# The gate's eight columns carried through the wide products of a graph, scan and expert kernel, and new banks and a new place for the heads' exponents

## What is computed

```python
x1 = x  + softmax(mask(leaky(s1 + s2.T), adj)) @ wh      # wh = LN(x) @ W, s = wh @ a
x2 = x1 + mamba2(LN(x1)) @ W_lin + b_lin                 # 8 heads, decay matrices exp(cs_i - cs_j)
x3 = x2 + sum_r (adj == r) @ LN(x2) @ weight[r] + bias   # 4 relations
logits = LN(x3) @ gate_w + gate_b                        # 8 experts
out = x3 + prob * expert(LN(x3))                         # top 1 with a capacity, 256 -> 1024 -> 256
```

## Time and profile before

| | |
|---|---|
| median of 3 runs | 3670.32 us (3669.29 to 3671.39) |
| profiled execution | 3668.25 us |
| its span, first to last instruction | 3666.5 us |
| mean granted TensorE clock | 0.99 of full speed |
| busy: PE / weight loads / DVE / ACT / POOL | 95% / 77% / 70% / 48% / 49% of the span |
| first phase, 64 graphs | 0 to about 2620 us, a pair of rounds in 79.8 us |
| second phase, 71 tiles | 2637 us to the end |

### The profile page before, as it was taken

How to read it: one execution, slowest core, us unless ns; L and a number is a source line. 1 busy time by engine, 2 the same in 40 slices (tenths; PEclk the granted TensorE clock), 3 DMA queues, 4 the chain that set the end, 5 groups by cost and what they waited for, 6 DMA issues and landing times.

```text
span 3666.5 us, 64685 instructions
## 1 busy us (share of the span) xinstructions
PE 3470.5 (95%) x20028; PEld 2838.1 (77%) x20028; DVE 2562.8 (70%) x7429; ACT 1776.8 (48%) x3627; POOL 1808.5 (49%) x2010
## 2 busy tenths in 40 slices
PE   7999999999999999999999999999699999999998
PEld 5777777777777777777777777777488888888887
DVE  5878888887888888788888878888444444444444
ACT  4556655655655555565565556555232323323232
POOL 3545554454554545545454554545354555545453
PEclk8999999999999999999999999999799999999999
DMA  3121111111111111111111111111155555556563
GB/s 104 39 46 36 35 40 43 37 42 41 37 38 40 40 37 46 37 37 40 37 42 35 46 37 37 40 38 33 58 199 194 196 190 193 193 192 197 194 196 128
DMA packets 166001, 301.92 MB, mean 82 GB/s; under 512 B 37376, under 2 KB 138240, under 8 KB 147776
## 3 DMA queue, kind: packets, MB, share of 16 engines
q0 software_dynamic: 38272, 196.40, 15.7%
q1 hardware_dynamic: 91536, 70.58, 6.3%
q10 hardware_dynamic: 36144, 34.35, 6.0%
HBM read 248.61 MB, written 52.65 MB: 82 GB/s over the span
## 4 chain that ended last, share of the span: by engine, by line
PE 51%; DVE 26%; POOL 12%; issue 8%; ACT 1%; DVEq 0%; DMA 0%; ACTq 0%; POOLq 0%; SPq 0%
PE bank L1337 13%; PE bank L1351 13%; PE bank L1083 7%; POOL masks L466 7%; DVE conv L798 6%; PE bank L1101 5%; PE bank L1189 4%; DVE y L966 3%; PE bank L1289 3%; DVE y L971 2%; POOL row L452 2%; POOL rstd L452 2%; DVE stats L779 2%; DVE xn L789 1%; PE bank L1220 1%
## 5 line engine op out<-in xcount | busy, mean ns | idle before, releaser
L732 ACT ACTIVATE decay<-bank,w_up 128x256 f32<-128x256 f32 x568 | 269.4, 474 | 700.3 <-PE bank L1337 694.5
L1083 PE MATMUL bank<-xn1T,w_in 128*128 128x256 f32 x2304 | 523.4, 381 | 15.3 <-issue 14.3
L1337 PE MATMUL bank<-zs,w_up 128*128 128x256 f32 x2272 | 504.6, 380 | 0.6 <-ACT zs L590 0.6
L1351 PE MATMUL bank<-w_dn,decay 128*128 128x256 f32 x2272 | 502.1, 379 | 0.0
L1101 PE MATMUL bank<-w_rel,hT 128*128 128x256 f32 x2048 | 492.7, 384 | 0.0
L1083 PEld LDWEIGHTS bank<-xn1T,w_in 128*128 128x128 f32 x2304 | 434.1, 190 | 72.3 <-issue 14.0
L798 DVE SCALAR_TENSOR_TENSOR conv<-bank,conv_w,conv 128x255 f32<-128x255 f32 (+2 forms) x960 | 461.3, 481 | 34.8
L1337 PEld LDWEIGHTS bank<-zs,w_up 128*128 128x128 f32 x2272 | 433.4, 191 | 60.3 <-issue 0.9
L1351 PEld LDWEIGHTS bank<-w_dn,decay 128*128 128x128 f32 x2272 | 426.2, 190 | 55.1
L1044 DVE TENSOR_TENSOR hT<-bank,w_dn 128x256 f32<-128x256 f32 x142 | 60.3, 424 | 537.1 <-PE bank L1351 537.1
L1101 PEld LDWEIGHTS bank<-w_rel,hT 128*128 128x128 f32 x2048 | 368.9, 190 | 62.8 <-ACT hT L590 13.0
(11 more groups left out here) (219 smaller groups left out, 6341.4 us busy)
## 6 DMA issues: line engine op xcount, KB each, us to landing
token_rows<-row SPq DMA_DIRECT2D x64, 258.0 KB, 2.7
xT_sb<-in_xT ACTq DMA_DIRECT2D x64, 256.0 KB
x_sb<-in_x ACTq DMA_DIRECT2D x64, 256.0 KB, 2.7
adj_sb<-in_adj SPq DMA_DIRECT2D x64, 256.0 KB, 3.0
adjt_sb<-in_adjT SPq DMA_DIRECT2D x64, 256.0 KB, 3.0
out<-row SPq DMA_DIRECT2D x64, 256.0 KB, 2.2
w_in<-token_rows,idc POOLq DMA_INDIRECT x142
out<-hT,ids POOLq DMA_INDIRECT x142
```

Source lines behind the costliest of these rows:

```text
L732: nc.scalar.activation(hid(f), bank[f % 4][:, 0:GROUP], ACT.Relu, bias=b1[q % 2][:, f:f + 1]).then_inc(hid_ready, 1)
L1083: ins = mm(dst, w_in[:, k, first:first + P], xn1T[:, k, :], start=k == 0, stop=k == DK - 1)
L1337: ins = mm(bank[f % 4][:, 0:GROUP], w1[i][:, k, f * P:(f + 1) * P], xgT[:, k, :], start=k == 0, stop=k == DK - 1)
L1351: ins = mm(bank[4 + j][:, 0:D], hid(f)[:, j * P:(j + 1) * P], w2[i][:, f, :], start=f == 0, stop=f == FB - 1)
```

## The change

Three things are done.

1. **The gate rides along.** A tile that held D = 256 columns now holds GX = 264 (x, x1, x1b, x2, x2b, wh, w_gat, w_lin, w_proj, w_rel, b_lin, b_rel, row). The eight further columns of each weight are that weight times the centred gate matrix, made once at the start with transposed copies of the weights. So x3's columns 256 to 263 are x3 @ gwc, and the logits come from two small DVE operations. xn3, its turns, xn3T and the gate product are gone. The DRAM row grows from 260 to 268 floats.
2. **Banks.** Each head has its own entry in EXPO; relate(1) goes to bank 7, the attention product to banks 0 and 1, the projection's second half to bank 2.
3. **Order.** `expo(range(0, 4))` stands in front of the turns of prob on the PE, and probT between decays 1 and 2 on ACT.

The core of the diff (loads, semaphores and slices `[..., 0:D]` left out):

```diff
-    EXPO = (2, 5, 3, 4)
+    EXPO = (2, 5, 1, 3, 4, 2, 5, 3)
...
-        WS = D + 2
+        WS = GX + 2 + E
...
         gat_loads = [
-            (w_gat, by_tile(io["L0_gnn_W"])),
+            (gate_w, by_tile(io["L1_ffn_gate_w"])),
+            (w_gat[:, :, 0:D], by_tile(io["L0_gnn_W"])),
+            (w_gatT, by_tile(io["gnn_WT"])),
             (a_bc, io["L0_gnn_a"].rearrange("(a d) o -> (a o) d", a=2).partition_broadcast(P)),
...
         # scalar engine
                     need(act, hp_made, b1_)
+                    need(act, x1_ready, b1_)
                     for t in range(T):
-                        ins = nc.scalar.activation(wh[:, t, :], bank[t][:, 0:D], ACT.Copy, scale=rstd[0][:, t:t + 1])
+                        copy(x[:, t, D:GX], bank[t][:, GX + 2:WS])
+                        ins = nc.scalar.activation(wh[:, t, :], bank[t][:, 0:GX], ACT.Copy, scale=rstd[0][:, t:t + 1])
...
-                    act.wait_ge(prob_turned, b1_ + 1)
-                    need(act, hp_made, b1_)
-                    copy(probT[:], bank[0][:, :]).then_inc(probT_ready, 1)
-                if b2_ is not None:
-                    for h in range(H):
+                for h in range(H):
+                    if h == 2 and b1_ is not None:
+                        act.wait_ge(prob_turned, b1_ + 1)
+                        need(act, hp_made, b1_)
+                        copy(probT[:], bank[0][:, :]).then_inc(probT_ready, 1)
+                    if b2_ is not None:
                         act.wait_ge(expo_made, 8 * b2_ + h + 1)
...
-                if b3_ is not None:
-                    act.wait_ge(xn3_turned, b3_ + 1)
-                    copy(xn3T[:], bank[7][:, :]).then_inc(xn3T_ready, 1)
...
         # vector engine
+                if is_first(b2_):
+                    dve.wait_ge(more_made, 1)
+                    v.tensor_copy(w_rel[:, :, :, D:GX], bank[6][:, REL:REL + R * DK * E].rearrange(
+                        "p (r k e) -> p r k e", r=R, k=DK))
+                    v.tensor_copy(w_proj[:, :, D:GX], ...).then_inc(more_ready, 1)
...
                 if b3_ is not None:
-                    need(dve, xn3_turned, b3_)
-                    normalise(3, xn3, row[:, :, 0:D], xn3_ready, b3_)
+                    dve.wait_ge(rstd_ready[3], b3_ + 1)
+                    for t in range(T):
+                        ins = v.scalar_tensor_tensor(lg[:, T * turn_[1] + t, :], row[:, t, D:GX], row[:, t, GX + 1:GX + 2],
+                                                     gate_b[:, t, :], ALU.mult, ALU.add)
+                    ins.then_inc(lg_in, 1)
...
-                    dve.wait_ge(gate_made, b3_ + 1)
                     g_, i, n = turn_
-                    ins = v.tensor_tensor(lg[:, T * i:T * (i + 1), :], bank[6]..., gate_b[:], ALU.add)
...
         # tensor engine, once, before the first product
+            for k in range(DK):
+                ins = mm(bank[6][:, 0:E], ones_row[:, 0:P], gate_w[:, k, :], start=k == 0, stop=k == DK - 1)
+            ins.then_inc(gate_sum_made, 1)
...
+            pe.wait_ge(gwc_ready, 1)
+            for i in range(DK):
+                for k in range(DK):
+                    ins = mm(bank[6][:, (1 + i) * E:(2 + i) * E], w_gatT[:, k, i * P:(i + 1) * P], gwc[:, k, :], ...)
+            ins.then_inc(gat_more_made, 1)
+            pe.wait_ge(gat_more_ready, 1)
+            for k in range(DK):
+                ins = mm(bank[4][:, D:GX], ones_row[:, 0:P], w_gat[:, k, D:GX], ...)
+            ins.then_inc(more_sum_made, 1)
...
                 if t == 0:
                     pe.wait_ge(xt_in, 16 * (b + 1))
-                    need(pe, probT_ready, b)
-                else:
                     need(pe, x1_ready, b)
...
-                    elif h in (2, 3):
-                        pe.wait_ge(xdt_ready, 2 * b + h - 1)
+                    elif h == 2:
+                        if b1_ is not None:
+                            pe.wait_ge(wh_ready, b1_ + 1)
+                    elif h in (3, 4):
+                        pe.wait_ge(xdt_ready, 2 * b + h - 2)
                     else:
-                        pe.wait_ge(decay_ready, 8 * b + h - 3)
+                        pe.wait_ge(decay_ready, 8 * b + {5: 1, 6: 2, 7: 4}[h])
...
         # in the rounds, after the turns of xs
-                if b3_ is not None:
+                if is_first(b2_):
+                    pe.wait_ge(lin_more_ready, 1)
+                    ...            # 8 products w_outT x w_lin[:, k, D:GX]
+                    pe.wait_ge(rel_in, 16 * len(rel_loads))
+                    ...            # 16 products w_relT x gwc
+                    ins.then_inc(more_made, 1)
+                if b3_ is not None:
+                    if b1_ is not None:
+                        pe.wait_ge(z_ready, b1_ + 1)
                     relate(1, range(0, 2))
+                if b2_ is not None:
+                    expo(range(0, 4), b2_, b1_)
                 if b1_ is not None:
                     pe.wait_ge(prob_ready, b1_ + 1)
                     ...            # turns of prob; in the first round then 4 + 4 products with gwc
-                if b2_ is not None:
-                    expo(range(0, 4), b2_)
                 if b3_ is not None:
                     relate(1, range(2, R)).then_inc(gy_made, 1)
...
+                    if b2_ is not None:
+                        pe.wait_ge(decay_ready, 8 * b2_ + 3)
                     for t in range(T):
                         for k in range(T):
-                            ins = mm(bank[1][:, t * D:(t + 1) * D], probT[:, k, t * P:(t + 1) * P], wh[:, k, :],
+                            ins = mm(bank[t][:, 0:GX], probT[:, k, t * P:(t + 1) * P], wh[:, k, :],
...
-                if b3_ is not None:
-                    pe.wait_ge(xn3_ready, b3_ + 1)
-                    if b1_ is not None:
-                        pe.wait_ge(z_ready, b1_ + 1)
-                    turn_pair(bank[7], xn3).then_inc(xn3_turned, 1)
...
-                if b3_ is not None:
-                    pe.wait_ge(xn3T_ready, b3_ + 1)
-                    for u in range(T):
-                        for k in range(DK):
-                            ins = mm(bank[6][:, u * E:(u + 1) * E], xn3T[:, k, u * P:(u + 1) * P],
-                                     gate_w[:, k, :], start=k == 0, stop=k == DK - 1)
-                    ins.then_inc(gate_made, 1)
```

More of the change, by code:

```diff
@@ L96, in sem @@
             return ctx.enter_context(nc.semaphore(name))
-        bank = [ctx.enter_context(nc.psum_tensor(f"bank{i}", [P, 512], F32)) for i in range(8)]
+        bank = [ctx.enter_context(nc.psum_tensor(f"bank{i}", [P, 512], F32)) for i in range(6)]
+        bank67 = ctx.enter_context(nc.psum_tensor("bank67", [P, 2, 512], F32))
+        bank += [bank67[:, i, :] for i in range(2)]
         rows_d = nc.dram_tensor("token_rows", [NT, ROW], F32, kind="Internal").ap()
@@ L150, in pair @@
             return sb(name, [P, 2, n], dt)
-        x = pair("x_sb")
+        x = pair("x_sb", F32, GX)
         adj = pair("adj_sb", I32, N)
@@ L159, in graph_mamba_moe @@
         emax, nmax, esum, rsum = sb("emax", [P, T]), sb("nmax", [P, T]), sb("esum", [P, T]), sb("rsum", [P, T])
-        x1, xn1, xn1T = pair("x1"), pair("xn1"), pair("xn1T", F32, N)
+        x1, xn1, xn1T = pair("x1", F32, GX), pair("xn1"), pair("xn1T", F32, N)
         stats = [sb(f"stats{i}", [P, T, 6]) for i in range(4)]
@@ L164, in graph_mamba_moe @@
         rstd = [sb(f"rstd{i}", [P, T]) for i in range(5)]
-        x1b = pair("x1b")
+        x1b = pair("x1b", F32, GX)
         conv = sb("conv", [P, CB, N])
@@ L182, in graph_mamba_moe @@
         y2h, y2s = sb("y2h", [P, 2, N]), sb("y2s", [P, N])
-        x2, x2b = pair("x2"), pair("x2b")
+        x2, x2b = pair("x2", F32, GX), pair("x2b", F32, GX)
         xn2 = pair("xn2")
@@ L193, in graph_mamba_moe @@
         row = sb("row", [P, T, ROW])
-        xn3, xn3T = pair("xn3"), pair("xn3T", F32, N)
         lg, lg2, ge, eq, rv = (sb(n_, [P, GT, E]) for n_ in ("lg", "lg2", "ge", "eq", "rv"))
@@ L204, in graph_mamba_moe @@
         tid = sb("tid", [P, GT], I32)
-        mv[3], rstd[3] = row[:, :, D:D + 2], row[:, :, D + 1]
+        mv[3], rstd[3] = row[:, :, GX:GX + 2], row[:, :, GX + 1]
         w_up = [sb(f"w_up_{i}", [P, WUP]) for i in range(2)]
@@ L220, in graph_mamba_moe @@
         w_row = sb("w_row", [P, TILES], I32)
-        idr, idr_f = x2b[:, 0, :].bitcast(I32), x2b[:, 1, :]
+        idr, idr_f = x2b[:, 0, 0:GROUP].bitcast(I32), x2b[:, 1, 0:GROUP]
+        gwc = w_gc[:, :, GX + 2:WS]
+        w_gatT, w_linT = (w_dn[1][:, i * DK * D:(i + 1) * DK * D].rearrange("p (k o) -> p k o", k=DK) for i in range(2))
+        w_relT = w_up[1][:, 0:R * DK * D].rearrange("p (r k o) -> p r k o", r=R, k=DK)
+        REL, PROJ = 320, 384
         ids, idc = sb("ids", [P, TG, P], I32), sb("idc", [P, TG, P], I32)
@@ L646, in step @@
                     for t in range(T):
```

(20 more changed lines are left out.)

130 lines of the change are left out of this document (86 added, 44 removed).

## The result

| | before | after |
|---|---|---|
| median | 3670.86 us (3669.29 to 3672.18) | 3729.11 us (3725.11 to 3734.02) |
| profiled execution, its span | 3668.25, 3666.5 us | 3725.11, 3723.4 us |
| mean granted clock | 0.99 | 0.972 |

The ratio is 1.0158 [1.0145, 1.0171]: 1.6% slower, 68 us above the forecast and 47 us above the end of its range.

A forecast was written before the change was run, and what follows sets the result against it. It took POOL's queue, then the DVE, to bound R rounds, the DVE most of Q, and PE the second phase. 3668.25 - 15.5 (pairs) + 11.1 (start) - 4.5 (end) = 3659.3, as median 3661 us; range 3645 to 3682.

The forecast's parts named there:

- The reading of R's end: End of an R round: POOL's queue runs without a pause to rstd[1], then the DVE's work sets the end.
- The start: Loads, gate sum and weight columns before and in the first rounds: +11.1 us (7 to 16).
- the end: The last graph's gate work, bare after the rounds, gets shorter: -4.5 us (-3.5 to -5).
- PE's work: Gate pieces removed, columns added: net -0.75 us per graph, but in the tail it becomes waiting, so booked 0.
- The middle of R: R rounds: earlier exponents and DVE multiplies, changed mask stretches on POOL: -0.3 us per pair, bounds 0 and -0.6.
- the caught case: Middle of R: third mask stretched beside the third multiply, rstd[3] then not; POOL ends about 0.1 us earlier.
- The tail: Between attend and projection: rstd[1] lighter without xn3 beside it, xn1 0.12 us earlier each round, -0.25 us per pair.
- The middle of Q: Q rounds: decays 0 and 1 earlier, 2 and 3 later: +0.05 us per pair, bounds -0.25 and +0.25.
- The sum of a pair: Steady pair of rounds: -0.5 us, bounds 0 and -0.9; over 31 pairs -15.5 us.
- Rival (B): Slower: ACT's copies delay POOL's queue, no stretched mask freed or Q gets one; +0.2 us per pair, 3683 us; chance 0.16.

The follow-up runs named there:

- e8: Changed kernel plus unused 256-column products, four ahead of the wait for xn1 and four behind its turns: 3696.0 us, ratio 1.0087.
- e16: Kernel before with only the new banks and order, and POOL's last mask behind the DVE's xn1: 3641.26 us, ratio 0.9928.
- e17: Changed kernel with e8's unused wide products and POOL's last mask behind xn1: 3663.12 us, ratio 0.9987.
- e18: Kernel before with POOL's last mask behind xn1: 3668.65 us, ratio 1.0003.
- e1: Changed kernel plus unused narrow products, four 128-column turns ahead of the turns of xn1, eight 8-column products behind: 3731.87 us, ratio 1.0175.
- e2: Changed kernel with POOL's last mask moved behind rstd[1]: 3734.31 us, ratio 1.0179.
- e7: Changed kernel with attend(1) moved behind the turns of xn1: 3725.66 us, ratio 1.0165.
- e4: Kernel before with only the new banks and order, gate and widths as before: 3681.26 us, ratio 1.0037.
- e6: Kernel before with POOL's last mask moved behind rstd[1]: 3689.54 us, ratio 1.0047.
- e10: Kernel before with attend(1) moved directly behind attend(0): 3667.92 us, ratio 1.0003.
- e11: Kernel before with only the new banks and order, and POOL's last mask behind rstd[1]: 3663.82 us, ratio 0.9981.
- e14: Changed kernel with only the first half of e8's products, those ahead of the wait for xn1: 3728.61 us, ratio 1.0166.
- e9: Changed kernel with e8's unused wide products and POOL's last mask moved behind rstd[1]: 3679.66 us, ratio 1.0039.

## Why the prediction was wrong, point by point

- **The reading of R's end.** The prediction has POOL work "without a pause" up to rstd[1], and so puts the last mask on the path. The timeline has POOL wait 0.18 us for the DVE there, and moving the mask in the kernel before gained nothing (79.86 us a pair against 79.92). The two engines were level, and whatever lengthened POOL's queue by more than 0.18 us had to show.
- **The start** (11.1 forecast, 13.3 measured, 12.5 by the columns alone) and **the end** (-4.5, -4.0) were right in kind and nearly in size. The second phase is unchanged, as forecast.
- **PE's work.** "What PE gains there is more waiting. I book 0." The first sentence held: ahead of the turns PE had waited 22.9 us in the window, for xn3, and now waits 36.7, for xn1; its wait for y went from 9.5 to 24.3. The zero is the step that failed most. More waiting with less work in it had a price of its own, the granted clock: 27 falls, some 30 us by e8. I had the granted clock at 1.00 in the window of the earlier trace rows and took it as given, though the change took products out of the one place where PE waits. No rival named it.
- **The middle of R** (-0.3, bounds 0 to -0.6). The DVE's gain is there: its wait at the first multiply fell by 1.2 us, and e16 shows 27 us over the run, 0.8 us a pair, more than my lower bound. But it did not get through, because POOL's queue grew by 0.5 us instead of shrinking. I saw that I could not say on which side the third mask falls, and bounded it at -0.1 for the caught case. What I left out is the tiny operation ("beats") ahead of the masks, at 0.19 us too small for a row, and caught for 0.72; and that two masks can be stretched in one round. The upper bound of the term should have been +0.5 at least.
- **The tail** (-0.25). rstd[1] did get lighter, 0.72 us instead of 0.83 in the R round and 0.77 instead of 0.82 in the Q round: 0.16 us of the forecast 0.25. That is already in the 12.8 us of POOL's queue above, which grew all the same. It wasn't tested alone.
- **The middle of Q** (+0.05, up to +0.25). Pairs without a fall split into 38.75 and 41.54 us where before had 39.06 and 40.85. So Q gained 0.3 and R lost 0.7, in spite of one stretched mask in Q, which POOL's slack took up (0.99 us before, 0.19 left). The forecast had the middle of R shorter and that of Q longer; it came out the other way round.
- **The sum of a pair** at full clock is +0.38 us, 12 us over the run, against -15.5. Rival (B) had a part of this mechanism, with its price: a mask stretched in Q too and none freed, +0.2 us a pair and 3683 us. With the clock held, the changed kernel takes 3696. The remaining 33 us no case had. Forecast and rivals together left out the one term that was the largest.

The size of the forecast, -0.5 us a pair, is nearly what e17 shows (79.37, -0.55), with the clock held and the mask out of the way: order -0.8 (e18 to e16), columns and filler +0.3 (e16 to e17). The agreement is luck in part, since the forecast's terms were others (-0.25, -0.3, +0.05) and it moved no mask. The gain of the earlier exponents was real; the forecast was wrong about both things that they met.

## What to carry to other kernels

Taking work from TensorE where it waits was not free here: look at the granted clock of that stretch, and after the change look at it first. Before an engine's step is moved earlier, lay the other engine's queue beside its new place, down to the operations of 0.2 us; a collision can move from one engine to the other. Where an order is right and the time says no, look for the one instruction that stands between two engines: here the place of a single mask made 40 us, from 3681 to 3641.

## What the runs showed of the hardware

- The falls of the granted clock from 2.4 to 1.2 GHz came in kernels whose PE was 92.6 to 95.5% busy from 1000 to 2000 us (after, e1, e2, e7), with waits of 2.1 us at most (e7 3.0). Others with 94.6 to 96.0% had none or one (before, e4, e6, e10, e11). A fall lasted 5 us in the mean (136.5 us for 27) and ended within the projection. What tells the kernels apart stays open, beyond what e1, e8 and e14 show.
- Less waiting did not mean fewer falls: e2 had 25.9 us of waiting for xn1 in the window instead of 36.7, and 56 falls instead of 27. Nor did as much waiting always bring them: e4, with the gate's products still in its tail, waited 33.8 us ahead of the turns and had none.
- A POOL operation of 0.19 us (128x1) took 0.91 us beside a DVE multiply with two SBUF inputs, and a mask 2.26 instead of 1.51: each time about +0.75, whatever its own length. The small one, held in after's R round, ended at 1574.42 us, 0.05 us behind the end of the multiply beside it.
- It can also be the multiply that is held. In Q rounds of e9 the second mask starts 0.03 us behind the second multiply (medians) and takes 2.28 us, the multiply 0.96; in those of e17 it starts 0.01 us behind it and takes 1.49, the multiply 1.43.
- A mask that started 0.03 us ahead of a DVE `tensor_scalar` stretched it from 0.74 to 1.06 us. Started beside the DVE's y instead (e16), the mask took 1.50 us, and the DVE's y and y*z took their 0.86 and 0.69 us, as in the kernel before.
